# Output products of the state space layer accumulated by token halves, and the last norm run by halves among them

## The reference, cut to what matters

```python
g = y * _silu(gate)                                        # 512 tokens x 2048
g = g * jax.lax.rsqrt(jnp.mean(g * g, axis=-1, keepdims=True) + EPS) * norm_w
x = x + jnp.einsum('bli,di->bld', g, W_out)                # 2048 -> 512
...
n = _layernorm(x, axis=-1)
logits = n @ gate_w                                        # 512 -> 8 experts, softmax, the best two
mid = jax.nn.silu(n @ Wg[e]) * (n @ Wu[e])                 # for each expert e
x = x + sum of We[:, e] * (mid @ Wd[e] + n @ A[e] @ B[e] * 2)
```

## Time and profile before

| | us |
|---|---|
| median of 3 timed runs | 1342.18 (1342.05 to 1343.96) |
| the profiled execution | 1341.35 |
| its span, first to last instruction | 1339.5 |
| PE busy | 1311.4 (98%) |
| DVE, POOL, ACT busy | 902.2, 662.1, 633.0 |

### The profile page before, as it was taken

How to read it: one execution, slowest core, us unless ns; L and a number is a source line. 1 busy time by engine, 2 the same in 40 slices (tenths; PEclk the granted TensorE clock), 3 DMA queues, 4 the chain that set the end, 5 groups by cost and what they waited for, 6 DMA issues and landing times.

```text
span 1339.5 us, 22005 instructions
## 1 busy us (share of the span) xinstructions
PE 1311.4 (98%) x8560; PEld 1077.8 (80%) x8560; DVE 902.2 (67%) x1413; ACT 633.0 (47%) x1307; POOL 662.1 (49%) x478
## 2 busy tenths in 40 slices
PE   8999999999999998999999999999999999999999
PEld 5677778778876665999999999999878888767887
DVE  5456766659668997778787777777446777563222
ACT  3534443353333435666666666666325446632111
POOL 3342477768737876153153252300565656535664
PEclk9999999999999999999999999999999999999999
DMA  4121223323333221000000001000231221312222
GB/s 156 51 76 49 58 84 95 94 74 93 94 112 132 73 61 32 1 27 26 1 27 26 1 26 38 21 1 3 76 110 49 79 80 64 95 40 88 94 94 79
DMA packets 31617, 83.15 MB, mean 62 GB/s; under 512 B 3488, under 2 KB 5664, under 8 KB 31264
## 3 DMA queue, kind: packets, MB, share of 16 engines
q1 hardware_dynamic: 31520, 81.81, 19.8%
HBM read 80.75 MB, written 1.05 MB: 61 GB/s over the span
## 4 chain that ended last, share of the span: by engine, by line
PE 89%; DVE 5%; ACT 3%; issue 1%; POOL 1%; DMA 0%; POOLq 0%; DVEq 0%
PE psum L930 24%; PE psum L931 23%; PE psum L932 23%; PE psum L1482 6%; PE psum L958 1%; PE psum L1000 1%; PE psum L1005 1%; PE psum L1001 1%; PE psum L1378 1%; PE psum L1416 1%; PE psum L1429 1%; PE psum L969 1%; PE psum L1685 1%; DVE xc L2275 1%; PE psum L1659 1%
## 5 line engine op out<-in xcount | busy, mean ns | idle before, releaser
L672 POOL TENSOR_SCALAR wpair<-landing 128x1024 fp32r<-128x1024 f32 (+3 forms) x115 | 102.7, 893 | 363.1 <-PE psum L932 199.1
L675 POOL TENSOR_TENSOR wpair<-landing,wpair 128x1024 fp32r<-128x1024 f32 (+3 forms) x115 | 221.8, 1929 | 9.6
L930 PE MATMUL psum<-xn,wpair 128*128 128x512 f32 x548 | 221.5, 404 | 0.4 <-POOL wpair L675 0.4
L931 PE MATMUL psum<-xn,wpair 128*128 128x512 f32 x548 | 216.1, 394 | 0.0
L932 PE MATMUL psum<-xn,wpair 128*128 128x512 f32 x548 | 215.4, 393 | 0.0
L2268 DVE TENSOR_TENSOR expo_t<-psum,expo_t 128x512 fp32r<-128x512 f32 (+1 forms) x224 | 144.5, 651 | 74.3 <-ACT expo_t L2042 70.8
L2042 ACT CAST expo_t<-psum 128x512 fp32r<-128x512 f32 (+1 forms) x224 | 124.3, 565 | 115.4 <-PE psum L1482 115.4
L930 PE MATMUL psum<-expo_t,kv_pair 128*128 128x256 f32 (+1 forms) x416 | 133.6, 321 | 0.2 <-DVE expo_t L2268 0.2
L1482 PE MATMUL psum<-const,expo 128*128 128x128 f32 (+1 forms) x832 | 127.6, 273 | 1.0 <-DVE expo_t L2268 0.6
L930 PEld LDWEIGHTS psum<-xn,wpair 128*128 128x128 f32 x548 | 102.9, 188 | 31.0 <-issue 7.0
L778 POOL TENSOR_TENSOR wpair<-landing,wpair 128x512 fp32r<-128x512 f32 x80 | 120.9, 1512 | 6.7
(11 more groups left out here) (328 smaller groups left out, 3020.5 us busy)
## 6 DMA issues: line engine op xcount, KB each, us to landing
landing<-in_weights SPq DMA_DIRECT2D x60, 512.0 KB, 3.3
landing<-in_weights SPq DMA_DIRECT2D x103, 256.0 KB, 2.7
kv<-in_ctx SPq DMA_DIRECT2D x8, 832.0 KB, 4.6
landing<-in_weights SPq DMA_DIRECT2D x15, 320.0 KB, 2.9
landing<-in_weights SPq DMA_DIRECT2D x16, 192.0 KB, 2.4
rotary_w<-in_rotary SPq DMA_DIRECT2D x1, 1920.0 KB, 9.1
rope_k<-in_rope_k SPq DMA_DIRECT2D x1, 1664.0 KB, 12.7
const<-in_constants SPq DMA_DIRECT2D x1, 1184.0 KB, 8.3
```

Source lines behind the costliest of these rows:

```text
L672: pool.tensor_scalar(wpair[:, slot, 0, 0:width], landing[:, slot, 0:width], 1.0, 1.0, ALU.mult, ALU.mult).then_inc(chunk_high, 1)
L675: pool.tensor_tensor(wpair[:, slot, 1, 0:width], landing[:, slot, 0:width], wpair[:, slot, 0, 0:width].bitcast(F32), ALU.subtract).then_in ...
L930: pe.matmul(out, w(0), act(0), start=start, stop=False)
L931: pe.matmul(out, w(0), act(1), start=False, stop=False)
```

## The change

All eight output chunks are summed as products of 256 columns, one token half at a time. In chunks 0 to 5 the two halves of a product stand next to each other. Chunks 6 and 7 are both held in their slots: chunk 6 for the first half, then chunk 7 for the first half, then both for the second half. The first half of the outputs is thus complete, is scaled and added to `x` and goes through the norm while the second half is still being summed. The norm's second half runs while PE works on the first half of stage F's opening tiles. The six matmuls of zeros are gone, the second half's squares move from DVE to ACT, the outputs are scaled and added by two tiles of half the tokens, and the squares of the gated values are taken one to two chunks earlier. The two tiles of `FB + 1` are done by halves too: their first halves among the norm, one second half ahead of `turn_logits`, the other behind it.

```diff
+        SQUARED_BEHIND = {3: (2,), 4: (3, 4), 5: (5, 6), 6: (7,), 7: ()}
+        HALF_BANKS = {5: (5, 7, 6, 5)}
...
+            def half_means(k, half):
+
+                for pair in range(2):
+                    pe.wait_ge(x_ready, 4 * (k - 1) + 2 * half + pair + 1)
+                    for f in (2 * pair, 2 * pair + 1):
+                        mm = pe.matmul(bank(HALF_BANKS[k][half])[:, 0:T // 2], mean_w[:, :], x[:, f, HALVES[half]],
+                                       start=f == 0, stop=f == FT - 1)
+                mm.then_inc(ln_mean, 1)
...
+            def half_tiles(half, m):
+
+                return bank(2 * half + m // 2)[:, (m % 2) * (T // 2):(m % 2 + 1) * (T // 2)]
...
+                def output_tile(c, kk, m, half):
+
+                    n = E_OUT + c
+                    return product(half_tiles(half, m), tile_of(n % 2, FT * kk + m),
+                                   lambda part: gated_pair[:, 2 * (c % 2) + kk, part, HALVES[half]],
+                                   start=c == 0 and kk == 0 and m % 2 == 0, stop=c == 7 and kk == 1 and m % 2 == 1)
...
                     for kk in range(2):
                         pe.wait_ge(gh_low, 2 * c + kk + 1)
                         for m in range(FT):
-                            if c == 7 and kk == 1 and m == FT - 1:
-                                means(5, (0,))
-                            mm = product(bank(m), tile_of(n % 2, FT * kk + m),
-                                         lambda part, kk=kk: gated_pair[:, 2 * (c % 2) + kk, part, :],
-                                         start=c == 0 and kk == 0, stop=c == 7 and kk == 1)
-                            if c == 7 and kk == 1 and m < FT - 1:
-                                mm.then_inc(e_out, 1)
+                            for half in range(2):
+                                mm = output_tile(c, kk, m, half)
                     mm.then_inc(chunk_used, 1)
...
-                for c in range(2, 8):
+                for c in range(2, 6):
                     output_chunk(c)
-                    if c == 6:
-                        square_means()
+                chunk_ready(E_OUT + 6)
+                pe.wait_ge(gh_low, 14)
+                output_half(6, 0, range(FT))
+                square_means()
+                chunk_ready(E_OUT + 7)
+                pe.wait_ge(gh_low, 16)
+                output_half(7, 0, (0, 1)).then_inc(e_out, 1)
+                output_half(7, 0, (2, 3)).then_inc(e_out, 1)
+                output_half(6, 1, (0, 1))
+                half_means(5, 0)
+                output_half(6, 1, (2, 3)).then_inc(chunk_used, 1)
+                for pair in range(2):
+                    half_square_sums(5, 0, pair)
+                output_half(7, 1, (0, 1)).then_inc(e_out, 1)
+                output_half(7, 1, (2, 3)).then_inc(chunk_used, 1)
...
-                layer_norm(5, 1)
                 pe.wait_ge(setup, 10)
                 chunk_ready(FB)
-                normal_tiles(5, [(bank(4)[0:NE, :], gate_tile(2), logits), (bank(0), slot_tile(FB % 2, 0), first),
-                                 (bank(1), slot_tile(FB % 2, FT), chunk_used)])
+                opening = [(bank(4)[0:NE, :], gate_tile(2), logits), (bank(0), slot_tile(FB % 2, 0), first),
+                           (bank(1), slot_tile(FB % 2, FT), chunk_used)]
+
+                def second_half_tile(m, half):
+
+                    for f in range(FT):
+                        mm = product(bank(2 + m)[:, HALVES[half]], tile_of((FB + 1) % 2, FT * m + f), half_tokens(half, f),
+                                     start=f == 0, stop=f == FT - 1)
+                    return mm
+
+                normal_group(5, 0, opening)
+                normal_group(5, 1, opening)
+                half_means(5, 1)
+                normal_group(5, 2, opening)
                 chunk_ready(FB + 1)
-                wide((FB + 1) % 2, 0, xn, bank(2)).then_inc(second, 1)
+                second_half_tile(0, 0)
+                for pair in range(2):
+                    half_square_sums(5, 1, pair)
+                second_half_tile(1, 0)
+                normal_group(5, 3, opening)
+                normal_group(5, 4, opening)
+                second_half_tile(0, 1).then_inc(second, 1)
                 turn_logits(2)
-                wide((FB + 1) % 2, FT, xn, bank(3)).then_inc(chunk_used, 1)
+                second_half_tile(1, 1).then_inc(chunk_used, 1)
...
+                if k in HALF_BANKS:
+                    deviation(0)
+                    for group in range(3):
+                        high(group)
+                    late_squares(0)
+                    late_squares(1)
+                    deviation(1)
+                    high(3)
+                    high(4)
+                    return
...
-                    if c < 7:
-                        gated_squares(c - 1)
-                    if c >= 6:
-                        gated_squares(c)
+                    for square in SQUARED_BEHIND[c]:
+                        gated_squares(square)
...
+            def layer_norm_by_halves(k, added):
+
+                dve.wait_ge(ln_mean, k + 1)
+                centre(k, 0, bank(HALF_BANKS[k][0])[:, 0:T // 2])
+                normalise(k, 0)
+                normalise(k, 1)
+                added(2)
+                normal_low(k, 0)
+                normalise(k, 2)
+                normal_low(k, 1)
+                added(3)
+                normal_low(k, 2)
+                dve.wait_ge(ln_mean, k + 2)
+                centre(k, 1, bank(HALF_BANKS[k][1])[:, 0:T // 2])
+                normalise(k, 3)
+                normalise(k, 4)
+                normal_low(k, 3)
+                normal_low(k, 4)
...
-                for m in range(FT):
-                    dve.wait_ge(e_out, m + 1) if m < FT - 1 else dve.wait_ge(chunk_used, E_OUT + 8)
-                    if m >= 2:
-                        dve.wait_ge(x_ready, 4 * 4 + m - 1)
-                    dve.tensor_tensor(y_sum[:, m % 2, :], bank(m), rstd[:, :], ALU.mult).then_inc(e_scaled, 1)
-                    dve.wait_ge(e_scaled, m + 1)
-                    dve.tensor_tensor(x[:, m, :], x[:, m, :], y_sum[:, m % 2, :], ALU.add).then_inc(x_ready, 1)
+                def outputs_added(b):
+                    half, pair = divmod(b, 2)
+                    dve.wait_ge(e_out, b + 1) if b < 3 else dve.wait_ge(chunk_used, E_OUT + 8)
+                    if half:
+                        dve.wait_ge(x_ready, 4 * 4 + pair + 1)
+                    scaled = y_sum[:, pair, :].rearrange("p (m t) -> p m t", m=2)
+                    dve.tensor_tensor(scaled, bank(b).rearrange("p (m t) -> p m t", m=2),
+                                      rstd[:, HALVES[half]].unsqueeze(1).broadcast_to([P, 2, T // 2]), ALU.mult
+                                      ).then_inc(e_scaled, 1)
+                    dve.wait_ge(e_scaled, b + 1)
+                    tiles = x[:, 2 * pair:2 * pair + 2, HALVES[half]]
+                    dve.tensor_tensor(tiles, tiles, scaled, ALU.add).then_inc(x_ready, 1)
+
+                outputs_added(0)
+                outputs_added(1)
 
             if runs("F"):
-                layer_norm(5)
+                layer_norm_by_halves(5, outputs_added)```

VectorE's list where the last outputs are added and the norm begins, in the kernel before (`y_sum` and `x` are the scaled output and the sum, `xc` the centred values, `xn` the high and low parts):

```order
L2967 TENSOR_TENSOR y_sum<-psum,rstd 128x512 [waits x_ready,chunk_used]
L2969 TENSOR_TENSOR x<-x,y_sum 128x512 [waits e_scaled]
L2275 TENSOR_TENSOR xc<-x,psum 128x2x256 [waits ln_mean]
L2275 TENSOR_TENSOR xc<-x,psum 128x2x256 x3
L2282 TENSOR_TENSOR sq<-xc 128x2x256 [waits ln_centred]
L2282 TENSOR_TENSOR sq<-xc 128x2x256
L2290 TENSOR_TENSOR xc<-xc,rstd 128x256 [waits ln_rstd] x2
L2268 TENSOR_TENSOR xn<-xc,xn 128x256 [waits ln_high]
```

More of the change, by code:

```diff
@@ new lines, in half_square_sums @@
+            def half_square_sums(k, half, pair):
+                if half:
+                    pe.wait_ge(ln_squared_late, 2 * (k - 1) + pair + 1)
+                else:
+                    pe.wait_ge(ln_squared, 2 * k + 2 + pair + 1)
+                for f in (2 * pair, 2 * pair + 1):
+                    mm = pe.matmul(bank(HALF_BANKS[k][2 + half])[:, 0:T // 2], mean_w[:, :], sq[:, f, HALVES[half]],
+                                   start=f == 0, stop=f == FT - 1)
+                if pair:
+                    mm.then_inc(ln_var, 1)
@@ new lines, in half_tiles, with normal_group @@
+            def half_tiles(half, m):
+                return bank(2 * half + m // 2)[:, (m % 2) * (T // 2):(m % 2 + 1) * (T // 2)]
+            def normal_group(k, group, tiles):
+                half, first_f, end_f = NORMAL_GROUPS[group]
+                pe.wait_ge(ln_high, 5 * k + group + 1)
+                for out, weights_of, _ in tiles:
+                    for f in range(first_f, end_f):
+                        w, act = weights_of(f), half_tokens(half, f)
```

(42 more changed lines are left out.)

59 lines of the change are left out of this document (19 added, 40 removed).

## The result

| | us |
|---|---|
| before, median of 6 runs beside the changed kernel | 1343.78 (1342.05 to 1344.77) |
| changed, median of 6 | 1350.74 (1347.67 to 1352.74) |
| ratio, 95% interval | 1.005 (1.0038 to 1.0062) |
| changed, 6 more runs on a second chip (before there 1343.27) | 1350.53 (1346.79 to 1352.49), ratio 1.0049 (1.0031 to 1.0067) |
| profiled execution of the changed kernel, its span | 1351.74, 1349.7 |

The change makes the kernel 7 us slower, more than the 2.7 that a measurement can tell. The forecast was 1343.4, and the range ended at 1345.8.

The account below looks back on a forecast made before the run. PE, busy 98% of the span, was taken as the bound. Waits 3.8 plus matmul-kind changes 0.6 replace 4.3; halving adds 1.0, rounding 0.2: +1.3, giving 1343.4, range 1340.6 to 1345.8.

Parts of the forecast that it names:

- Halving: Output chunks as 256-column products: chunk 5.71 instead of 5.59, 0.7 over chunks 0 to 5, 0.3 for 6, 7, FB + 1.
- The rival with slower half-width products: Long runs of half-width products: 0.124 each instead of 0.119, 2.2 more, 1345.6; chance 0.08.
- Step 4: Chunk 7's second half, then groups 0 and 1: PE waits 0.25 for DVE's low part, not for POOL's splits.
- The stage's sum: Stretch from POOL's start on chunk 7 to PE's first product of FB + 3; forecast 41.3.
- four short waits: PE waits for chunk 7's split 0.25, first half means 0.2, first square sums 0.25, second half means 0.1.
- the changes between fp32 and product matmuls: PE's switches of matmul kind in the new order: about 0.05 to 0.1 at each of ten, some 0.6.
- Step 6: After the second half's square sums: one half tile (1.43) covers a chain of 2.4, PE waits 1.25 for the high part.
- step 8: Turned logits to turned rows: PE waits about 1.5 for DVE's gate chain; POOL no longer waited for ahead of FB + 3.
- The square mean's sum: Sum of 15 adds, whole over 4 us ahead of the square mean, not waited for; up to 1.5 if late.
- The clock rival: PE's rests in the norm and gate waits lower the clock to 1.2 GHz: 4.3 more, 1347.7; chance 0.06.
- The forecast's sign: In the profile after, a granted-clock slice under full would show the prediction wrong.

Follow-up runs that it names:

- order mended: Changed kernel with POOL's split of FB + 1 held until the first half's low parts are written, late square sums then both FB + 1 first-half tiles after group three; 1343.51.
- logits first: Changed kernel with turn_logits(2) ahead of second_half_tile(0, 1) instead of behind it; 1349.05, ratio 1.004.
- both: Changed kernel with the order mended and also the logits turned first; 1343.84, ratio 1.0003.

## Why the prediction was wrong

- **Halving (+0.7 ahead of chunk 6, 0.3 behind): right, a little less.** 5.68 a chunk instead of 5.71, so 0.5 ahead of chunk 6. The rival with slower half-width products fell.
- **Step 4 is the one that failed.** It had `FB + 1` split by 1185.4 and the normalising and low parts of groups 0 and 1 from 1180.7 to 1182.35 and on, with durations from the earlier trace rows, and said of the splits that "neither is waited for". That is so, and beside the point. In the kernel before POOL splits `FB + 1` from 1177.85 to 1182.08, and is idle when DVE normalises and takes low parts; there the rows are of DVE undisturbed. My own times put the two side by side, and I did not ask what the one does to the other. The waits came to 1.30 + 1.87 in place of 0.25. The kernel before with the split moved shows it by itself (+2.3), and the changed one with it moved away gets the durations back.

  The trace of the kernel before held the sign, in rows that I had not taken up: this split meets two of DVE's adds from SBUF. POOL's instructions take 1.49 and 2.66 instead of 1.05 and 2.41, and the second add 0.81 instead of 0.69.

```profile
1178.35 0.68 DVE L2967 TENSOR_TENSOR y_sum<-psum,rstd 128x512 f32<-128x512 f32 x1
1179.07 0.81 DVE L2969 TENSOR_TENSOR x<-x,y_sum 128x512 f32<-128x512 f32 x1
```

```profile
1177.85 1.49 POOL L672 TENSOR_SCALAR wpair<-landing 128x1024 fp32r<-128x1024 f32 x1 [4.23 <-issue]
1179.42 2.66 POOL L675 TENSOR_TENSOR wpair<-landing,wpair 128x1024 fp32r<-128x1024 f32 x1
```

- **The stage's sum.** At full clock the stage was 44.1, the forecast had 41.3. The waits that the profile lists (3.2 + 1.0 + 1.4) are 5.6 against 3.0 in the forecast (0.25 + 1.25 + 1.5), which is 2.6 of the 2.8. The rest of the stage is 38.5 against 38.3, with four short waits (0.8) and the changes between fp32 and product matmuls (0.6) in the forecast. Two of the short waits can be seen though the profile does not list them: POOL ends the split of chunk 7 at 1173.34 and PE's first product of it starts at 1173.40, 0.23 behind the point where the square mean's 0.86 would be over (forecast 0.25), and the first square sums start 0.2 late (0.25). The changes of kind cost more at fewer places: the first product behind a mean or a square sum holds PE for 0.31 (1179.61 to 1179.92 in the changed kernel's timeline) where the others take 0.12, at four places (all four at 0.30 or 0.31 in the second profile, whose clock is full there), 0.8 in all; I had taken 0.05 to 0.1 at each of ten.
- **Step 6 (0.96 for 1.25) and step 8 (1.37 for 1.5): right**, mechanism and size, and both could be taken away by more work in front. Step 8's other half, that POOL would no longer be waited for ahead of `FB + 3`, was right too. The square mean's sum was in time.
- **The clock rival, 0.06: it occurred, elsewhere and smaller.** It was placed behind steps 6 and 8 at 4.3. The fall came behind the two waits for DVE, in two of the six profiles that have them bare (the changed kernel and the logits first), at 1.4 and 1.6. In both profiles with zeros in these waits it did not come. Two out of two is no proof when the bare ones lack it in four of six. The forecast's sign, a slice of the clock under full, did show, but that slice is the one with the wait at 414 us.
- **The ledger against 7.0:** 0.5 of halving and 3.4 of the stage, shown, and some 0.5 of clock at the stage on average (1.4 and 1.6 in two of six). The remaining 2.6 lies ahead of anything that the change touches. Its kind, a landing that comes late and a half clock behind PE's rest, is seen in the kernel before too.

The timed runs say more, since each has its mean granted clock on record. A straight line through 51 runs of the kernel before gives 1.2 us for each 0.001 of clock, with a scatter of 0.8; it covers the late waits too where they come with a lower clock. Against this line, that is at equal clock, each kernel comes out near what its stage, the halving and the rest behind the stage add up to:

| kernel | runs | slower than before at equal clock | by stage, halving and the rest behind it |
|---|---|---|---|
| changed | 12 | 4.2 | 3.9 |
| halved products alone | 12 | 1.2 | 0.6 |
| before, split late | 12 | 2.2 | 2.0 |
| changed, split late | 10 | 2.6 | 1.9 |
| changed, zeros | 6 | 4.2 | 3.9 |
| changed, logits first | 7 | 3.9 | 3.4 |
| order mended | 12 | -0.8 | -0.6 |
| both | 12 | -0.9 | -1.1 |

What is left of the 7.0 goes with the clock. The mean is 0.9963 in the changed kernel's runs and 0.9984 in before's, and none of the 12 has 1.000, which 20 of the 51 have; the seven other kernels lie between (0.9977, 11 of 71). This is hardly chance: 12 runs drawn at random from these 63 have so low a mean in under one of 1000 draws, though the runs come from three chips. Only some 0.5 us of it is at the stage. Why the changed kernel runs at a lower clock where its instructions are still those of before stays open.

## What to carry to other kernels

Moving an engine's step in time changes who runs beside it. Take a duration from the trace only with the neighbour that it had there, and for VectorE steps with two SBUF inputs look at what GpSimd does in the same microseconds; a transfer or a split that nobody waits for can still be what makes the critical chain late. An instruction that takes longer than its usual time in the trace, as POOL's 1.49 for 1.05 did before the change, is the sign to look for. The mend was to hold a split that was early anyway until the chain was through, and to place work that waits for nothing in PE's list where it covers the longest chain. And when two versions differ by little, compare a stretch between two rows that does not change from run to run (here 40.7 in four profiles), and the runs at equal mean clock, beside the whole time.

## What the hardware showed that I had not expected

- DVE and POOL take turns instruction by instruction: a 0.42 step of DVE took 1.26 or 2.56 and a 0.69 step 2.85, according to which of POOL's two instructions (1.05 and 2.41) was under way; POOL's own first took 1.50 behind a DVE add.
- The clock fell behind waits of 1.30 and 1.87 in two of six profiles of the same instructions with the same waits. Behind the wait of 3.23 at 414 us it fell in all seven profiles that have it, of before and of changed kernels alike, and at the same place behind waits of 2.38 and 2.55; in the eight profiles with 1.73 or less there it stayed full.
- A load's landing at about 410 us made PE's wait there 1.44, 1.72, 2.38, 2.55 or 3.23, and none in one profile of before, though the kernels are the same up to it.
